# Delta-rule block and feed-forward on one core: inverses, gate weights and filter inputs moved between stages

## The reference

```python
q = short_conv(x @ Wq.T, conv_q); k = ...; v = ...       # 4 taps, then silu
beta = sigmoid(x @ Wb.T)                                 # one per token and head
# delta rule in chunks of 32 tokens, q and k divided by their norms
A = where(tri_strict, -(kbc @ swapaxes(kc, -1, -2)), 0)  # kb = k * beta
T = solve_triangular(eye - A, eye, lower=True)           # a 32x32 inverse per chunk and head
u = T @ vc; w = T @ kbc; then the scan over the chunks
local_s, local_m, local_l = fir(v, 3), fir(v, 15), fir(v, 63)   # per channel filters
logits = einsum('bld,hpd->blhp', x, gate_w) + gate_b
probs = softmax(logits / exp(log_temp)) * (1 - 5 * eps) + eps
o = probs0*local_s + probs1*local_m + probs2*local_l + probs3*delta_out + probs4*v
x = layernorm(x + rmsnorm(o, norm_w).reshape(...) @ Wo.T)
x = layernorm(x + ffn(x))                                # hidden size 1024, three layers
```

## Time and profile before

| | us |
|---|---|
| median of 3 runs | 2274.93 (2270.86 to 2278.68) |
| profiled execution | 2272.73 |
| its span, first to last instruction | 2270.9 |
| projection | 0 to 358.8 |
| gate weights and filters | 358.8 to 575.9 |
| delta rule and feed-forward | 575.9 to 2270.9 |

### The profile page before, as it was taken

One profiled execution on the slowest core, in us unless ns is written; L12 is line 12 of the kernel. 1 busy time (PEld: TensorE's weight loads), 2 busy tenths in 40 slices (PEclk: granted clock), 3 DMA queues, 4 the chain that ended last, 5 costly groups with the idle time before them and its releaser, 6 DMA issues.

```text
span 2270.9 us, 41455 instructions
## 1 busy us (share of the span) xinstructions
PE 2067.6 (91%) x16936; PEld 1753.8 (77%) x16936; DVE 1163.6 (51%) x1803; ACT 884.8 (39%) x1438; POOL 521.0 (23%) x530
## 2 busy tenths in 40 slices
PE   7888882778699999599999999999999999999998
PEld 5776762667588887488888888888888888888886
DVE  5777776974377776334334434434433443443442
ACT  4455541110244444234434434434443443443442
POOL 1111777875355555100000000000000000000000
PEclk9999995798699999699999999999999999999999
DMA  5666667677999996100000000000000000000000
GB/s 166 195 195 167 209 181 195 222 220 276 211 233 236 238 236 161 60 1 28 1 28 28 1 28 28 1 28 28 6 23 28 29 1 28 28 1 28 28 1 19
DMA packets 246751, 217.02 MB, mean 96 GB/s; under 512 B 158786, under 2 KB 210498, under 8 KB 241986
## 3 DMA queue, kind: packets, MB, share of 16 engines
q1 hardware_dynamic: 234306, 184.29, 29.6%
q10 hardware_dynamic: 12288, 30.41, 4.5%
HBM read 130.52 MB, written 84.15 MB: 95 GB/s over the span
## 4 chain that ended last, share of the span: by engine, by line
PE 56%; DVE 1%; issue 1%; ACT 1%; DMA 0%; POOLq 0%; DVEq 0%; SPq 0%; POOL 0%; ACTq 0%
PE B L1534 50%; PE O L1561 5%; PE T L1492 1%; DVE yb L1667 0%; ACT gate L1606 0%; DMA srow<-in_srow 0%; DVE stats L1695 0%; DVE stats L1729 0%; ACT L1606 0%; DVE x L1690 0%; DVE z L1720 0%; DVE xl L1647 0%; DVE z L1724 0%; DVE x L1708 0%; DVE z L1743 0%
## 5 line engine op out<-in xcount | busy, mean ns | idle before, releaser
L1620 ACT ACTIVATE yb<-B,scol 128x512 f32<-128x512 f32 x256 | 176.7, 690 | 580.2 <-PE B L1534 580.2
L1534 PE MATMUL B<-act1l,wr 128*128 128x512 f32 x1024 | 398.5, 389 | 0.0
L1534 PE MATMUL B<-act0h,wr 128*128 128x512 f32 x1024 | 398.3, 389 | 0.0
L1534 PE MATMUL B<-act0l,wr 128*128 128x512 f32 x1024 | 398.3, 389 | 0.0
L1534 PE MATMUL B<-act1h,wr 128*128 128x512 f32 x1024 | 398.3, 389 | 0.0
L1655 DVE TENSOR_TENSOR act0l<-yb,act0h 128x512 fp32r<-128x512 f32 x256 | 176.2, 688 | 317.4 <-ACT act0h L1623 315.2
L453 DVE SCALAR_TENSOR_TENSOR acc<-proj,taps,acc 128x512 f32<-128x512 f32 x288 | 214.7, 750 | 84.4 <-ACT acc L399 75.8
L1655 DVE TENSOR_TENSOR act1l<-yb,act1h 128x512 fp32r<-128x512 f32 x128 | 88.6, 692 | 295.5 <-ACT act1h L1623 295.5
L1534 PEld LDWEIGHTS B<-act0l,wr 128*128 128x128 f32 x1024 | 192.2, 188 | 39.9
L1534 PEld LDWEIGHTS B<-act1l,wr 128*128 128x128 f32 x1024 | 192.2, 188 | 39.9
L1534 PEld LDWEIGHTS B<-act1h,wr 128*128 128x128 f32 x1024 | 192.2, 188 | 39.9
(11 more groups left out here) (169 smaller groups left out, 3204.0 us busy)
## 6 DMA issues: line engine op xcount, KB each, us to landing
qk_s<-yT SPq DMA_DIRECT2D x16, 1024.0 KB, 6.1
kk_s<-kfull SPq DMA_DIRECT2D x16, 1024.0 KB, 6.4
qk<-qk_s SPq DMA_DIRECT2D x32, 512.0 KB, 4.2
wraw<-in_ffn_w ACTq DMA_DIRECT2D x32, 352.0 KB, 5.0
toe<-in_toe_short ACTq DMA_DIRECT2D x32, 320.0 KB, 7.4
xt<-in_xt SPq DMA_DIRECT2D x16, 524.0 KB, 4.3
k_s<-ktok SPq DMA_DIRECT2D x16, 512.0 KB, 7.2
v_s<-vtok SPq DMA_DIRECT2D x16, 512.0 KB, 3.2
```

Of the source, the lines that this page charges most:

```text
L1534: last = nc.tensor.matmul(B[slot % 4][:, :], w, part, start=(k == 0 and i == 0), stop=(k == kts - 1 and i == len(parts) - 1))
L1620: last = nc.scalar.activation(dst, B[slot % 4][:, :], ACT.Gelu, scale=scol[:, slot:slot + 1])
```

## The change

1. **Parts.** `tri` is divided by steps into four parts of two slots instead of two halves of four. GpSimd inverts parts 0 and 1 in the projection, part 0 in steps 6 to 9, part 1 in steps 10 to 14, with the scaled rows. VectorE inverts parts 2 and 3 together (four slots, as many elements as its half before) in the filter stage. Its 60 operations stand behind groups 4 to 55, `(n - 4) * 15 // 13` of them before group `n`: one per group, two in every eighth or so.
2. **Key products** are made for chunks of 64 tokens: 32 matmuls of 64x64 per step in one go behind block 0, two ScalarE copies instead of four, `kk_s` half as large.
3. **Logits.** Behind steps 4, 8 and 12 the logits of four steps are prepared and exponentiated, one step later the shares are computed; only the last four steps' stay in the filter stage. The scales of a part are made behind steps 4 and 8.
4. **Filter inputs.** The window of head 0 (`win0`) is filled by SP from `vtok` in each step, and the first three tables are loaded by ScalarE's queue at the start of the kernel; GpSimd zeroes their unused part there.
5. TensorE's, ScalarE's and VectorE's loops over steps are written out.

```diff
-EARLY_COLS = {10: (1, 5), 11: (5, 9), 12: (9, 12), 13: (12, 15), 14: (15, 18), 15: (18, 21), 16: (21, 25)}
+PARTS = 4
+EARLY = 2
+EARLY_COLS = {6: (0, 1, 8), 7: (0, 8, 14), 8: (0, 14, 20), 9: (0, 20, 31),
+              10: (1, 1, 8), 11: (1, 8, 14), 12: (1, 14, 20), 13: (1, 20, 27), 14: (1, 27, 31)}
...
+                    sp.dma_start(win0[:, NT + t * BATCH:NT + (t + 1) * BATCH, :], vtok[p][:, 0, :, :]).then_inc(v_stored[p], 16)
+                    sp.dma_start(win0[WIN:P, t * BATCH:(t + 1) * BATCH, :], vtok[p][0:WIN, 0, :, :]).then_inc(v_stored[p], 16)
+                    if t + 1 < STEPS:
+                        sp.dma_start(win0[0:WIN, (t + 1) * BATCH:(t + 2) * BATCH, :], vtok[p][WIN:P, 0, :, :]).then_inc(v_stored[p], 16)
...
-                    squared(t, p, 0)
-                def squared(t, p, first):
-                    if first:
-                        pe.wait_ge(kk_out, t * 4 + 2)
...
+                    for s in range(BH):
                         b, hh = s // KT, s % KT
+                        for chunk in HALVES:
+                            for par in range(2):
+                                kt = yT[p][64 * par:64 * par + DK, KT + hh, b * P + chunk.start:b * P + chunk.stop]
+                                last = nc.tensor.matmul(side[par][chunk, s * HC:s * HC + HC], kt, kt, start=True, stop=True)
+                    last.then_inc(kk_ready, 1)
...
-                after = {0: keys, 1: lambda t, p: squared(t, p, 2), 2: small, 4: values}
+                after = {0: keys, 2: small, 4: values}
...
             def _(act):
+                for n in range(NTOE):
+                    toeplitz(act, io, keep, n)
...
+                for t in range(1, STEPS):
+                    step(t, t % 2, (t - 1) // 2, True, t < 2)
+                    if t % PART_STEPS == 0:
+                        c = t // PART_STEPS - 1
+                        act.wait_ge(small_out, t + 1)
+                        if c < EARLY:
+                            if c:
+                                act.wait_ge(gam0_done, c)
+                            nc.scalar.activation(ebeta[:, :, :], raw[:, c * NE:c * NE + NE, NGATE:NGATE + HEADS], ACT.Exp,
+                                                 scale=-1.0).then_inc(exp0_done, 1)
+                        act.wait_ge(to_exp0, c + 1)
+                        nc.scalar.activation(lg0[:, :, :, :], lg0[:, :, :, :], ACT.Exp).then_inc(exp0_done, 1)
...
+                for t in range(1, STEPS):
+                    step(t, t % 2, (t - 1) // 2, True)
+                    if t % PART_STEPS == 0:
+                        first_logits(t // PART_STEPS - 1)
+                        if t // PART_STEPS <= EARLY:
+                            first_scales(t // PART_STEPS - 1)
+                    if t % PART_STEPS == 1 and t > 1:
+                        first_shares(t // PART_STEPS - 1)
...
+        D_OUT, T_OUT = {2: 0, 6: 1, 29: 2, 30: 3}, {4: 0, 8: 1, 30: 2, 31: 3}
+        TURNS = {2: (0,), 5: (1,), 28: (2, 3)}
...
+                sub = Substitution(nc.vector, keep, EARLY, outer, LATE)
                 for n in range(NGRP):
                     weigh(n)
-                    if n < COLS:
-                        link(sub.outer_product(n + 1))
-                        link(sub.update(n + 1))
-                    if n == COLS:
+                    if n == 1:
...
+                        sub.scaled_columns().then_inc(columns_scaled, 1)
+                        dve.wait_ge(columns_scaled, 1)
+                    if n == 2:
+                        query_scales()
+                    if SUB_FIRST <= n < SUB_END:
+                        for i in range((n - SUB_FIRST) * 15 // 13, (n - SUB_FIRST + 1) * 15 // 13):
+                            link(sub.update(i // 2 + 1) if i % 2 else sub.outer_product(i // 2 + 1))
+                    if n == SUB_END:
                         dve.wait_ge(upper_zero, 1)
+                        sub.scaled_rows().then_inc(keep["inv_done"][1], 1)
```

More of the change, by code:

```diff
@@ L402, in step @@
                             keys_out(t - 1, 1 - p, n)
-                        if follow and cb == 1:
-                            squared_out(t - 1, 1 - p, 2)
+                        if follow and cb == 3:
+                            scales_out(t - 1)
                         if cb >= 1:
@@ L515, in _ @@
                 nc.gpsimd.memset(zero[:, :, :], 0.0).then_inc(zeroed, 1)
+                nc.gpsimd.memset(win0[0:WIN, 0:BATCH, :], 0.0)
+                for i in range(NTOE):
+                    nc.gpsimd.memset(toe[i][0:SHORT, 0:NF - 1, :, :], 0.0).then_inc(keep["toe_zero"], 1)
                 pool.sem_inc(sqk_done, 2)
-                sub = Substitution(nc.gpsimd, keep, 0, keep["outer0"])
                 def squares(t, p):
@@ new lines, in toeplitz, with by_matrix @@
+def toeplitz(act, io, keep, n):
+    toe, toe_in = keep["toe"][n % NTOE], keep["toe_in"][n % NTOE]
+    act.dma_start(toe[:, NF - 1, :, :], io["toe_long"][n]).then_inc(toe_in, 16)
+    act.dma_start(toe[SHORT:, 0:NF - 1, :, :], io["toe_short"][n]).then_inc(toe_in, 16)
+def by_matrix(nc, gam, half):
+    for par in range(2):
+        last = nc.vector.tensor_copy(gam[:, :, par, :],
+                                     half.rearrange("p (v b) (k r) -> p v r (b k)", b=GB, r=2)[:, :, par, :])
+    return last
@@ L560, in weights_fir, with turn_scales @@
+def turn_scales(nc, out, gam, ident, parts=1):
+    for c in range(parts):
+        for rows in HALVES:
+            last = nc.tensor.matmul(out[rows, c * HC:c * HC + HC],
+                                    gam[rows, c * 2 * PART_STEPS:(c + 1) * 2 * PART_STEPS, :, :].rearrange("p t r s -> p (t r s)"),
+                                    ident[rows, rows], start=True, stop=True)
+    return last
 def weights_fir(nc, sems, io, keep):
@@ L726, in _, with turn @@
-                for n in range(NTOE):
-                    toeplitz(n)
-                nc.scalar.activation(itemp[:, :], prm[:, NGATE:NGATE + HEADS], ACT.Exp, scale=-1.0).then_inc(exps, 1)
-                nc.scalar.activation(beta[:, :, :], raw[:, :, NGATE:NGATE + HEADS], ACT.Exp, scale=-1.0).then_inc(exps, 1)
+                def turn(c):
+                    inverses_there(act, c)
+                    if c >= 2:
+                        act.wait_ge(turned_stored[c % 2], 64 * (c // 2))
+                    nc.scalar.activation(turned_inv[c % 2][:, :, :, :],
+                                         tri[:, c * PSLOTS:c * PSLOTS + PSLOTS, :, :].rearrange("p q i c -> p q c i"),
+                                         ACT.Copy).then_inc(turned, 1)
@@ L777, in _ @@
-                link(nc.vector.reciprocal(half[:, :, :], half[:, :, :]))
-                for par in range(2):
-                    last = nc.vector.tensor_copy(gam[:, :, par, :], streams(half[:, :, :])[:, :, par, :])
-                last.then_inc(gam_done, 1)
-                link(nc.vector.tensor_scalar(eps[:, :], prm[:, NGATE + HEADS:NGATE + 2 * HEADS], 0.0, 0.2, ALU.max, ALU.min))
-                link(nc.vector.tensor_scalar(slope[:, :], eps[:, :], -5.0, 1.0, ALU.mult, ALU.add))
-                dve.wait_ge(exps, 3)
@@ L1877 @@
     "v_s": (HEADS, P, STEPS + 1, BATCH, DK),
[L1878 removed]
+    "kk_s": (P, GRP, HC),
     "f_s": (GRP, NQ, CH, CH),
```

402 lines of the change are left out of this document (197 added, 205 removed).

## The result

The changed kernel took 2245.6 us (median of 4 runs, 2239.27 to 2255.0), the kernel before 2276.8 (4 runs, 2270.86 to 2282.82): ratio 0.9873, 95% interval 0.9843 to 0.9903. The profiled execution took 2246.64, its span is 2244.8. The forecast was 2223 (2220.9 profiled). The change is faster, clear of noise but by 1.3% instead of the 2.3% forecast: 26 us of span instead of 52.

The account below looks back on a forecast made before the run. The projection was bound by a TensorE-ScalarE-VectorE loop with no engine full, the filter loop's first 30 groups by VectorE. Terms summed to -51.8 us: 2272.7 to 2220.9 profiled, 2223 median; 8-in-10 range 2205 to 2247.

Parts of the forecast that it names:

- Logits and scales in the projection: Projection: three logits events instead of one, mostly hidden in existing gaps; +2.2 us, between 0 and +6.
- Key products by chunks: Projection steps: 64-column key matmuls at 35 ns let the third product start earlier; 0.62 us less per step, -9.3 us.
- End of the projection: Projection's end: wait chain loses its middle, -2.8 us; last stores instead of GpSimd end the stage, -2.4 us.
- Start: Kernel start: three filter tables issued while TensorE waits for its first input; +3 us, bounds 0 and 7.4.
- Head: Filter stage before the first weighing: only a quarter of the logits left, 9.0 us instead of 35.8; -26.8 us.
- Loop: Filter loop: substitution spread over 52 groups, stalls 21.8 us, late tables 4; 155.6 us instead of 172.8, -17.2 us.
- Rival C: Filter loop: GpSimd's two additions become the bound at 3.61 us a group; slower, 2284 us; chance 0.03.
- B: Filter loop: TensorE bounds the spread loop if its clock stays low; +24, 2247 us; chance 0.13.
- Tail: Last weighing to next stage: the last two parts' turns and stores make 8.4 us some 10; +1.5 us.
- D: Projection: the chunks bring no shorter step, matmuls taking 72 ns; +13.8, 2237 us; chance 0.13.
- E: Loop and start: no added stalls (-9.2), no late tables (-4), a free start (-3); 2207 us; chance 0.12.

Follow-up runs that it names:

- no_reload: Changed kernel with filter tables loaded only for the first three parts and reused, output not the reference's; 2232.56 us in a single run.
- spread2: Changed kernel with the logits work spread over four steps, one logits operation behind each step's small copies; 2218.92 us, ratio 0.9776 to the kernel before.
- adds_out: Changed kernel without three quarters of GpSimd's two additions in the last 32 of 64 loop groups, output not the reference's; 2233.84 us, single run.
- split: Changed kernel with key products issued in two halves again, the second waiting for ScalarE's copies; 2242.38 us, ratio 0.9882 to the kernel before.
- toe_late: Changed kernel with the first three filter tables issued in projection steps 1 to 3 instead of at the start; 2239.5 us, ratio 0.9871 to the kernel before.
- spread: Changed kernel with logits, scales and shares cut into pieces over four steps, in larger pieces than the later version; 2226.23 us, ratio 0.9799 to the kernel before.

## Why the prediction was wrong, and where it was right

**Logits and scales in the projection** is the step that failed: +2.2 forecast, with 0 to +6 as bounds, +25.9 measured, 23.7 of the 25.7 us by which the profiled execution missed the forecast. I added up work ("over the gap that is there anyway", "the reload falls under TensorE's third product") and took the durations of TensorE's and VectorE's rows as constants. The three events cost 10.6, 10.7 and 9.6 us, and the rows of after divide them, if each us by which a row is longer counts as one:

| event, us | TensorE's rows behind the gaps, over normal | VectorE's blocks of logits and shares, over the first event's | rest |
|---|---|---|---|
| first | 7.5 | 0 | 3.1 |
| second | 2.9 | 4.5 | 3.2 |
| third | 3.4 | 2.0 | 4.1 |
| sum | 13.8 | 6.5 | 10.4 |

The rest is the work itself, 10.4 for the 7.0 that I had. TensorE's part in the first event is 1.83, 0.79, 0.77, 0.15, 2.35 and 1.57 in the rows shown. That such a us costs nearly one is shown there: in no_reload 5.8 us less of them make the event 5.4 shorter without any edit. In spread2 the four intervals from 88.27 on hold the whole first event for 0.8 us. VectorE's part stands in the two events in which GpSimd has column operations, and in the three cases given above VectorE's operation ends some 0.35 us behind GpSimd's; no version removed GpSimd's operations from an event, so this column rests on the rows, and on adds_out, which shows the effect in the loop. Both are estimates from rows and not prices that an experiment took away one by one.

The kernel before had a warning that I did not read: its one event had the second half of the key products in TensorE's gap. Part 2 of the change took that filler away while part 3 made the gap longer, and I priced the two apart. What the filler was worth is not shown (split).

The Trainium skill (TensorE: Matmul & The Clock Gate, section on HAM oscillation) says that idle stretches between bursts send the engine back to the half rate. This trace agrees, 2.03 to 3.86 us behind 3.92 idle, and shows what that costs where the products are on the loop. It isn't so behind every gap: in no_reload 2.82 us idle were followed by products of 2.03.

**Key products by chunks**: -0.80 us a step instead of -0.62. The mechanism came as forecast, with the third product starting when VectorE frees its buffer, but it needs only the narrower chunks and not their merging (split). The records took 18 ns, not 35. I misread: that row stands behind 19.62 us of idle time at a granted clock of 0.50. The same line at the full clock has 0.69 us for 32, 22 ns a record. Window and timeline of before:

```profile
586.00:587.20 1.20, 1.15 (x38) 1.15 (x40) 0.00 (x0) 0.00 (x0) 0.00 (x0) 0.50 1.32 181
```

```profile
615.57 0.69 PE L1031 MATMUL Q<-qk 64*64 64x64 f32 x32
```

So even the first price in the forecast held the lower clock, and I did not look at the level beside the row.

**End of the projection**: -3.0 for -3.4. The stage's end behind VectorE's was 5.0 us, in my bounds of 2 to 5.7 but not at my 3.3: -0.8 for -2.4.

**Start**: +2.7 for +3 at the first copy, 4.2 at the first product. The tables cause 2.3 of the first copy's (toe_late).

**Head**: 9.5 us for 9.0.

**Loop**: 155.5 for 155.6, which is luck: two errors cancel. The stalls of VectorE's substitution operations were 64.8 - 50.4 = 14.4 us, not 21.8; the waits for tables 18.4 us, not 4, and no_reload prices them at 9.2 on the path. Rival C is out: GpSimd's pair took 2.1 us a group (1303 and 803 ns). B is out as well, with the clock over the loop higher than the 0.83 of the earlier trace rows, in this window of after:

```profile
394.00:516.00 122.00, 99.64 (x396) 94.07 (x396) 104.82 (x106) 8.22 (x2) 104.33 (x99) 0.92 0.88 264
```

**Tail**: 13.2 for 10, the inverses' turns at 4.1 us each and their stores in front of the last values.

D (no shorter step) and E (nothing late) did not happen, and none of the rivals named what did. That 2245.6 lies within the wide range of 2205 to 2247 is luck too: its upper end was rival B's.

## What to carry to other kernels

Work that is added to an engine's gap in a tight loop costs its own time, what TensorE loses behind a longer idle stretch, and what VectorE's small operations lose beside GpSimd's. Read the granted clock and the duration of a repeated matmul row before and behind each gap, and price what follows the gap at the lower rate as the worse case. Look at the clock beside every row that you take a price from. Cut such work into pieces that fit gaps which exist, and ask of each edit what it takes out of a gap that another edit widens. Earlier work in a loop helps only if its buffers allow it: the earlier end alone gave nothing, with a fourth table buffer the loop kept its length and the end stayed short.

## What the runs showed of the hardware

Matmuls of 64x64 by 64 columns, with inputs and outputs alternating over the two halves of the partitions, took 18 ns a record at the full clock (1.16 us for 64) and 35 ns at a granted clock of 0.50 (1.13 us for 32); 64x128 by 128 columns took 72 ns in the earlier trace rows.

The same gap of 3.92 us was followed by 12 us at a granted clock of 0.50 with TensorE busy throughout in one run, and by the full clock some 4 us later in another. The first event varies by over 5 us between runs of the same code.

A VectorE operation with two inputs in SBUF of 0.49 us took up to 3.20 beside one of GpSimd's, and ended 0.35 us behind it: 221.52 + 3.20 against 220.73 + 3.64 in spread2, 185.15 + 2.07 against 184.72 + 2.14 in spread. Beside GpSimd's column operations of some 1.0 to 1.3 us it took 0.57 to 1.29 (second event of after).
